# Softmax sums of 16 heads in one block, one reciprocal a batch, spread through DRAM; another opening order

## What is computed

```python
qp = q @ Wq.T
k, v = jnp.split(latent_kv @ Wkv_expand.T, 2, axis=-1)
scores = jnp.einsum('bhqd,bhkd->bhqk', qh, kh) * inv_sqrt_d
scores = jnp.where(causal, scores, jnp.finfo(scores.dtype).min)
attn = jax.nn.softmax(scores, axis=-1)
out = jnp.einsum('bhqk,bhkd->bhqd', attn, vh)          # heads concatenated after this
x = _layernorm(x + out @ Wout.T, axis=-1)
```

## Time and profile before

| | us |
|---|---|
| median of 3 runs (lowest to highest) | 1207.15 (1203.7 to 1211.64) |
| the profiled execution, device time | 1207.56 |
| its span, first to last instruction | 1205.9 |
| cross attention in it, about 288 to 626 | 338 |
| step 0, first `below_peak` to `attend(0)` (340.95 to 363.17) | 22.2 |
| step t = 1, start of `attend(0)` to `attend(1)` (363.17 to 399.30) | 36.1 |
| steps t = 2..5, from 399.30 to 548.29 | 149.0 |
| steps 6 and 7 | 31.3, 26.3 |

### The profile page before, as it was taken

How to read it: one execution, slowest core, us unless ns; L and a number is a source line. 1 busy time by engine, 2 the same in 40 slices (tenths; PEclk the granted TensorE clock), 3 DMA queues, 4 the chain that set the end, 5 groups by cost and what they waited for, 6 DMA issues and landing times. The chain is left out here.

```text
span 1205.9 us, 19206 instructions
## 1 busy us (share of the span) xinstructions
PE 1083.9 (90%) x6786; PEld 913.0 (76%) x6786; DVE 732.0 (61%) x1552; ACT 445.4 (37%) x795; POOL 286.2 (24%) x380
## 2 busy tenths in 40 slices
PE   5999999998498889887758969999999999899997
PEld 4788888886487677776636848999989999787785
DVE  3746374562676786677554746776767777434575
ACT  4614233242143333433325224555545555221210
POOL 4510101004222332223325211122111221223030
PEclk9999999999789999888888989999999999999998
DMA  4402020304878668564216137667766676432241
GB/s 148 167 1 105 0 104 0 104 0 153 247 219 229 180 179 215 159 168 132 72 58 213 31 118 251 220 226 244 241 241 214 230 236 214 139 106 94 80 140 70
DMA packets 88820, 179.33 MB, mean 149 GB/s; under 512 B 8032, under 2 KB 33632, under 8 KB 87104
## 3 DMA queue, kind: packets, MB, share of 16 engines
q1 hardware_dynamic: 82096, 155.06, 40.2%
q0 software_dynamic: 6672, 23.60, 5.8%
HBM read 136.95 MB, written 41.42 MB: 148 GB/s over the span
## 5 line engine op out<-in xcount | busy, mean ns | idle before, releaser
L45 PE MATMUL e_ps_h<-e_x_lo,e_gu_hi 128*128 128x256 f32 (+1 forms) x552 | 156.2, 283 | 5.0 <-DVE e_x_lo L1722 5.0
L46 PE MATMUL e_ps_h<-e_x_hi,e_gu_lo 128*128 128x256 f32 (+1 forms) x552 | 154.1, 279 | 0.0
L47 PE MATMUL e_ps_h<-e_x_hi,e_gu_hi 128*128 128x256 f32 (+1 forms) x552 | 154.0, 279 | 0.0
L45 PE MATMUL a_ps_proj<-a_x_lo,arena 128*128 128x512 f32 x256 | 102.8, 401 | 15.1 <-DVE a_x_lo L295 12.2
L740 DVE CUSTOM_DVE_ANT_0 b_dump<-b_ps_s,b_mask 128x128 f32<-128x128 f32 (+1 forms) x256 | 79.7, 352 | 55.7 <-PE b_ps_s L924 55.2
L45 PEld LDWEIGHTS e_ps_h<-e_x_lo,e_gu_hi 128*128 128x128 f32 (+1 forms) x552 | 99.6, 180 | 6.2 <-DVE e_gu_lo L1726 5.2
L309 DVE SCALAR_TENSOR_TENSOR a_xc<-a_ps_proj,a_taps,a_xc 128x510 f32<-128x510 f32 (+2 forms) x96 | 71.6, 746 | 53.4 <-ACT a_xc L268 51.1
L46 PE MATMUL a_ps_proj<-a_x_hi,arena 128*128 128x512 f32 x256 | 102.1, 399 | 0.0
L47 PE MATMUL a_ps_proj<-a_x_hi,arena 128*128 128x512 f32 x256 | 102.1, 399 | 0.0
L46 PEld LDWEIGHTS e_ps_h<-e_x_hi,e_gu_lo 128*128 128x128 f32 (+1 forms) x552 | 99.7, 181 | 1.0
L47 PEld LDWEIGHTS e_ps_h<-e_x_hi,e_gu_hi 128*128 128x128 f32 (+1 forms) x552 | 99.7, 181 | 0.0
(11 more groups left out here) (294 smaller groups left out, 2741.2 us busy)
## 6 DMA issues: line engine op xcount, KB each, us to landing
f_gate_up_raw<-we_gate_up SPq DMA_DIRECT2D x88, 352.0 KB, 4.8
qk_split<-arena SPq DMA_DIRECT2D x32, 512.0 KB, 4.8
b_sk<-qk_split SPq DMA_DIRECT2D x48, 256.0 KB, 4.1
b_sq<-qk_split SPq DMA_DIRECT2D x48, 256.0 KB, 5.5
f_down_raw<-we_down SPq DMA_DIRECT2D x23, 512.0 KB, 3.8
y_slots<-f_y_tile SPq DMA_DIRECT2D x23, 512.0 KB, 2.8
f_x_next<-x SPq DMA_DIRECT2D x6, 1024.0 KB, 6.4
f_down_raw<-we_down SPq DMA_DIRECT2D x23, 192.0 KB, 3.9
```

What stands on the lines that cost most here:

```text
L45: pe.matmul(out, a_hi, b_lo, start=first, stop=False)
L46: pe.matmul(out, a_lo, b_hi, start=False, stop=False)
L47: return pe.matmul(out, a_hi, b_hi, start=False, stop=last)
```

## The change

- `attend`: all row sums of a batch are computed first, 32 matmuls with weights `pick[:, c]`, whose ones stand in every fourth column from c on. Head h of chunk c adds its sums into partitions h*32 + c, h*32 + c + 4, ... of one 128x256 block in `ps_x`. Then 64 values x exp matmuls fill both blocks of `ps_o` with no wait on `normalize`.
- VectorE takes one reciprocal of 128x256 a batch (`invert`) instead of four. SP stores it to DRAM (`inverse`) and reads it back four times, each time 4 rows copied to 32 partitions, into `share` (128 x 4 x 256). This is `share_inverse(t-1)`, first in SP's step t.
- ScalarE copies the unnormalised output from PSUM to `a_raw` (`keep`); VectorE multiplies it by `share` in two halves of 128x512, in the next step at u = 0, i = 2 and 3. `a_hi` and `a_lo` follow in halves on ScalarE (i = 2, 3) and GpSimd (i = 4, 5). PE's `out` waits for them.
- `peaks(t, 1)` moves from i = 1 to i = 4 on PE and ScalarE, to i = 5 on VectorE. SP's place for its transfer stays.
- Opening: the statistics move behind `turned(1, 1)`; the four normalising instructions go to ScalarE at the end of step -1; batch 1's context is rounded a step earlier; GpSimd's memset of `sk` comes earlier.
- `split_stored` and `m_loaded` become single semaphores; `m_hi` and `m_lo` share a tile.

```diff
+            def share_inverse(b):
+                sp.wait_ge(rinv_done, b + 1)
+                sp.dma_start(inverse_dram, rinv[:]).then_inc(share_loaded, 16)
+                sp.wait_ge(share_loaded, 80 * b + 16)
+                if b:
+                    sp.wait_ge(a_raw_done, 2 * b)
+                for h in range(HC):
+                    rows = slice(h * HD, (h + 1) * HD)
+                    sp.dma_start(share[rows], inverse_dram[h * HD:h * HD + HC].rearrange("(o c) t -> o c t", o=1)
+                                 .broadcast_to([HD, HC, S])).then_inc(share_loaded, 16)
...
             for t in range(FIRST_T, END_T):
+                if 1 <= t <= B:
+                    share_inverse(t - 1)
                 if 0 <= t - 2 < NORMED:
...
                         cut(t, u, i)
+                        if t and u == 0 and i in (4, 5):
+                            rest(t - 1, i - 4)
...
+            def keep(b):
+                for u in range(2):
+                    act.wait_ge(sums_o_ready, o_count(b, u))
+                    if b:
+                        act.wait_ge(a_lo_done, 2 * (b - 1) + u + 1)
+                    act.activation(a_raw[:, UC * u:UC * u + UC].rearrange("p c t -> p (c t)"), ps_o[:, u], ACT.Copy)\
+                        .then_inc(o_kept, 1)
+
+            def attended(b, u):
+                act.wait_ge(a_raw_done, 2 * b + u + 1)
+                if b:
+                    act.wait_ge(out_ready, 2 * b)
+                cs = slice(UC * u, UC * u + UC)
+                act.activation(a_hi[:, cs], a_raw[:, cs], ACT.Copy).then_inc(a_hi_done, 1)
...
                     if t == -1:
+                        act.wait_ge(ln_step, TILES + 7)
+                        for k in range(TILES):
+                            act.activation(res[:, k], res[:, k], ACT.Identity, scale=left_ln.rstd[:, k:k + 1],
+                                           bias=left_bias[:, k:k + 1]).then_inc(normed_done, 1)
                         peaks(0, 0)
...
-                        if i == 1 and u == 0:
+                        if i == 4 and u == 0:
                             peaks(t, 1)
...
+                        if t and u == 0 and i in (2, 3):
+                            attended(t - 1, i - 2)
+                keep(t)
...
-            def normalize(b, c):
-                dve.wait_ge(o_ready, DC * b + c + 1)
-                if b:
-                    dve.wait_ge(a_lo_done, DC * (b - 1) + c + 1)
-                dve.reciprocal(rinv[:, c % 2], ps_o[:, c % 2, S:2 * S]).then_inc(rinv_done, 1)
-                dve.wait_ge(rinv_done, DC * b + c + 1)
-                dve.tensor_tensor(a_raw[:, c], ps_o[:, c % 2, 0:S], rinv[:, c % 2], ALU.mult).then_inc(a_raw_done, 1)
+            def invert(b):
+                dve.wait_ge(sums_o_ready, sums_count(b))
+                if b:
+                    dve.wait_ge(share_loaded, 80 * b)
+                dve.reciprocal(rinv[:], ps_x[:, 0, 0:S]).then_inc(rinv_done, 1)
+
+            def normalize(b, u):
+                dve.wait_ge(share_loaded, 80 * (b + 1))
+                dve.wait_ge(o_kept, 2 * b + u + 1)
+                a = a_raw[:, UC * u:UC * u + UC].rearrange("p c t -> p (c t)")
+                dve.tensor_tensor(a, share[:, UC * u:UC * u + UC].rearrange("p c t -> p (c t)"), a, ALU.mult).then_inc(a_raw_done, 1)
...
             def out(b, k, part):
                 t = b + 1
+                pe.wait_ge(a_lo_done, 2 * b + part + 1)
...
             def attend(b):
                 pe.wait_ge(cut_done, HEADS * (b + 1))
+                for c in range(DC):
+                    for r in range(BT):
+                        for h in range(HC):
+                            mm = pe.matmul(ps_x[h * HD:(h + 1) * HD, 0, r * P:S], pick[:, c],
+                                           pt[:, HC * c + h, 2 * r * P:(2 + r) * P],
+                                           start=c == 0 and r == 0, stop=c == DC - 1 and r == BT - 1)
+                mm.then_inc(sums_o_ready, 1)
                 pe.wait_ge(v_done, 2 * b + 2)
```

More of the change, by code:

```diff
@@ L410, in cross_attention @@
         mask = sb("mask", [P, 3 * P])
-        ones = sb("ones", [P, HD])
+        pick = sb("pick", [P, HC, HD])
+        share = sb("share", [P, DC, S])
         x_hi = sb("x_hi", [P, DC, S], F32R)
@@ L584, in cut, with rest @@
                                    pattern=[[0, 2], [1, P]], channel_multiplier=-1).then_inc(cut_done, 1)
-            def rest(b, c):
-                pool.wait_ge(a_hi_done, DC * b + c + 1)
-                pool.tensor_tensor(a_lo[:, c], a_raw[:, c], a_hi[:, c].bitcast(F32), ALU.subtract).then_inc(a_lo_done, 1)
+            def rest(b, u):
+                pool.wait_ge(a_hi_done, 2 * b + u + 1)
+                cs = slice(UC * u, UC * u + UC)
+                pool.tensor_tensor(a_lo[:, cs], a_raw[:, cs], a_hi[:, cs].bitcast(F32), ALU.subtract).then_inc(a_lo_done, 1)
             context(0)
@@ L598, in _ @@
                                    fill=MASKED, base=0, pattern=[[-1, P]], channel_multiplier=1).then_inc(consts, 1)
[L599 to L600 removed]
+            for c in range(HC):
+                pool.memset(pick[:, c, c:HD:HC], 1.0).then_inc(consts, 1)
+            pool.wait_ge(consts, 10)
             context(1)
@@ L613, in _ @@
                     pool.tensor_tensor(bln.rstd[:], bln.var[:], bln.power[:], ALU.pow).then_inc(rstd_done, 1)
-                for c in range(DC):
-                    rest(t, c)
+            for u in range(2):
+                rest(B - 1, u)
         @block.scalar
@@ L666, in fill @@
                         if i == 0:
-                            context(b)
+                            if b != 1:
+                                context(b)
                             turned(b, 0)
@@ L670, in fill @@
                             turned(b, 1)
+                            if b == 0:
+                                context(1)
                         if i == 2:
@@ L702, in _ @@
                             peaks(t + 1, 0)
-                for c in range(DC):
-                    act.wait_ge(a_raw_done, DC * t + c + 1)
-                    if t:
-                        act.wait_ge(out_ready, 2 * t)
-                    act.activation(a_hi[:, c], a_raw[:, c], ACT.Copy).then_inc(a_hi_done, 1)
+                        if t and u == 0 and i in (2, 3):
+                            attended(t - 1, i - 2)
+                keep(t)
+            for u in range(2):
+                attended(B - 1, u)
         @block.vector
@@ L797, in fill @@
                             norm_step(o, i - 3)
-            def left_sums():
-                moments(dve, res, left_ln, ln_step, 0, var_done)
-                dve.wait_ge(rstd_done, 1)
-                for k in range(TILES):
-                    dve.tensor_scalar(res[:, k], res[:, k], left_ln.mean[:, k:k + 1], left_ln.rstd[:, k:k + 1],
-                                      ALU.subtract, ALU.mult).then_inc(normed_done, 1)
             for u in range(2):
@@ L825, in _ @@
                         fill(t, u, i)
-                        if u == 0 and i == 1:
+                        if t and u == 0 and i in (2, 3):
+                            normalize(t - 1, i - 2)
+                        if u == 0 and i == 5:
                             peaks(t, 1)
@@ L829, in _ @@
                             peaks(t + 1, 0)
-                for c in range(DC):
-                    normalize(t, c)
+                invert(t)
+            for u in range(2):
+                normalize(B - 1, u)
             for k in range(BT):
@@ L955, in attend @@
                         pe.wait_ge(m_lo_done, 2 * b + 2)
[L956 removed]
+                    if c == UC and real(b + 1):
                         pe.wait_ge(m_lo_done, 2 * b + 3)
[L958 to L967 removed]
+                    if c % UC == 0 and b:
+                        pe.wait_ge(o_kept, 2 * (b - 1) + c // UC + 1)
+                    for r in range(BT):
+                        for h in range(HC):
+                            head = HC * c + h
+                            mm = pe.matmul(ps_o[h * HD:(h + 1) * HD, c // UC, c % UC * S + r * P:(c % UC + 1) * S],
+                                           v[:, b % 2, r, head * HD:(head + 1) * HD], pt[:, head, 2 * r * P:(2 + r) * P],
+                                           start=r == 0, stop=r == BT - 1)
+                    if c % UC == UC - 1:
+                        mm.then_inc(sums_o_ready, 1)
             def fill(t, u, i):
```

83 lines of the change are left out of this document (44 added, 39 removed).

## The result

| | before | after |
|---|---|---|
| median, us (lowest to highest) | 1205.68 (1203.70 to 1211.64) | 1252.76 (1248.02 to 1254.42) |
| the profiled execution, us | 1207.56 | 1248.02 |
| its span, us | 1205.9 | 1246.1 |
| last output projection begins, us | 617.41 | 657.38 |

The changed kernel is slower: ratio 1.0375, 95% interval 1.0327 to 1.0424. (The median of before is over four runs here; the table ahead of the prediction had three of them.) The profiled execution of after is the lowest of its four, so differences read from the two traces add up to 40.5 us where the medians stand 47.1 apart. All 40.0 us of the traces' difference are there when the last output projection begins, so the loss is inside cross attention.

What follows compares the result with a forecast made beforehand. PE, busy 90%, was taken to bound the kernel; the change adds a loop through SP of 11.6 + 11.8 + 14.2 + 5.2 = 42.8 us. Delays 38.9 + 3 + 2.6 = 44.5 on 1207.5 give 1252 us, range 1220 to 1268.

Steps and rivals of the forecast that it cites:

- term 1: SP's list, from the low part of peaks (t, 1) done to the first stack load: 11.6 us (10.7 to 12.4).
- term 2: SP's list, from the first to the second stack load of a step: 11.8 us, not getting shorter.
- term 3: From second stack load to `share` landed, the inverse store queued behind six stack pieces: 14.2 us (12.5 to 15.7).
- term 4: VectorE and ScalarE work from `share` landed to the low part of the next peaks: 5.2 us (4.7 to 6).
- tail: After `attend(7)` to the last projection: 14.1 us against 11.5 before, so +2.6 us.
- The loop through SP: Cross attention: peaks wait for `share`, `share` for SP behind stack loads, those for earlier peaks; 42.8 us for 36.5 us steps.
- Step 0: First cross-attention step, with two residuals queued: peaks to stack load 13.4 us, next peaks at 396.1.
- small transfers overtake: Rival: the round trip's small transfers pass the stack loads, each of six rounds 4.2 us shorter, 1227 us; chance 0.15.
- the round trip is hidden: Rival: `share` at most 8.6 us behind the stack load, so the kernel is faster, 1180 us; chance 0.11.
- The wait at the product: VectorE waiting on a DMA before its product with `share`: near 10 us in steps 1 to 6.
- The opening: Before step 0: PE's 13.44 us wait goes, but SP waits for `normed_done` before the stack load; gains about nothing.
- step 7: Cross-attention step with an empty queue: 16.2 us from `attend` to `out`, against 13, so +3 us.

## Why the prediction was right

The forecast was 1252 us in a range from 1220 to 1268, with 0.79 on slower by over 1%; the median is 1252.76. Its steps against the trace:

| | predicted | measured |
|---|---|---|
| term 1, peaks to first stack load | 11.6 | 10.6, 10.5 |
| term 2, first to second stack load | 11.8 | 12.1 |
| term 3, second stack load to `share` | 14.2 | 13.7 |
| term 4, `share` to the peaks | 5.2 | 5.2 |
| sum, steps 2 and 3 | 42.8 | 41.6, 42.0 |
| peaks (0, 1) issued | 351.5 | 353.77 |
| peaks (1, 1), (2, 1), (3, 1) | 396.1, 436.7, 479.5 | 397.83, 438.08, 479.72 |
| peaks (4, 1), (5, 1) | 522.3, 562.7 | 521.76, 561.78 |
| `out(5, 0, 0)` | 602.8 | 601.23 |
| tail, `attend(7)` to the last projection | 14.1 | 13.4 |

- **The loop through SP** is what the runs show. That the four terms add up to the step is no proof, since they are cut out of one round. What shows it is that in steps 1 to 6 of after SP never waits for the inverses, that nothing but the trip's place in SP's list changed where 46 us came back, and that SP then waits for the inverses in every step. Making the peaks early shortens the loop too, by 22 us in all.
- **Term 1** was 1 us too large, with 10.6 just under my lower bound of 10.7: the residual lands 6.4 us after its issue in this step, where it took 7.9 in the one stretch that I took the queue's pace from the earlier trace rows. With 0.5 us too much in term 3 it makes the steps 0.4 to 1.2 us shorter than forecast.
- **Step 0** was missed by 2.3 us: the late peaks (0, 1) go out at 353.77. They also make `attend(0)` start at 370.79, against 363.17 before and 361.94 with the peaks early. I had not priced this step. Its first term I put at 13.4, where the rows that I named add up to 13.9 (1.5 and 12.4); it measured 13.0. Behind it SP's loop takes over, and the five steps that were each a little shorter than forecast had used up the 2.3 us by the peaks (5, 1).
- **Term 3, the queue in order.** The store lands 5.8 us after its issue, behind the six pieces, as counted (9.7 less 3.9). Two small errors cancel in it: the row's 5.6 us is the median of two pieces, and the last one took 6.0 by itself (6.0 in after too), while the store follows it by 0.4 us and not by 0.8. The half microsecond too much is in the loads, which land 2.2 us behind their last issue (472.34 to 474.54), where I took 3.0. The rival "small transfers overtake" (1227) needed a landing within 3 us and is refuted; so is "the round trip is hidden" (1180), which needed `share` at most 8.6 us behind the stack load. The price of the Trainium skill's page "DMA: Bandwidth & Descriptors", section "Anatomy of one DMA", would have made term 3 9.5, as an estimate; the page gives it for transfers issued by GpSimd, and here SP issues. It is near what an empty queue shows: by it a store of 128 KB takes 2.3 us, and the last two stores of after land in 1.7 and 2.0; the whole trip would take 5.5, and took 5.8 with the trip first. The backlog has to be added.
- **The wait at the product** was foretold near 10 us in steps 1 to 6. It is 10.4 in the first and 5.5 to 7.3 in the other five: the place was right, the size was not.
- **The opening** gains nothing: measured by itself, ratio 0.9989. The reason that I gave (the stack load (1, 0) a little later) is in the trace, 330.14 against 328.36. The experiment with the store moved shows more: without SP's wait it would still not start before 326.4.
- **The clock.** I had the lower clock only at the upper end of the range. It fell, from 0.955 to 0.936 over the span. The trace cannot say what that cost.
- **The sum.** The traces stand 40.0 us apart at the last projection, the medians 47.1; my 44.5 lies between, so the agreement with the median to a microsecond is partly luck. Against the traces I was 4.5 too high: 1.6 at `out(5, 0, 0)` (+37.3 for +38.9), 2.3 behind it (up to `attend(7)` the loss grows by 0.7, to +38.0, where I had 3 for step 7), and 0.6 in the tail. Step 7 is the term of the sum that was mis-sized most: from `attend(6)` at 616.76 to its output projection at 631.48 are 14.7 us, not 16.2, and PE makes up most of the rest by `attend(7)`.

## What to carry to other kernels

Before adding a wait to an engine that issues transfers, write down everything that engine has to issue between this wait and the same wait of the next step, and follow it round through the engines that release it: where each idle stretch of the issuing engine is one of the loop's own waits, the sum of that loop, not the busy time, is the new step. A dependent round trip through memory belongs ahead of bulk transfers, in issue order and in time; here its place before or behind six loads of 256 KB was worth 46 us, or 30 with the peaks early. A second queue did not get round the backlog here, since its transfers meet the same transfer engines: 1242 us with it, 1207 with the trip first on the one queue.

## What was not expected of the hardware

- The backlog holds a small transfer up on another queue as well: a store of 128 KB landed in 5.2 us on ScalarE's own queue, with the stack pieces of SP's queue in flight, against 5.8 on SP's queue and 1.7 to 2.2 with two pieces or nothing in flight.
- Two pieces of 256 KB put ahead of four loads of 128 KB, with four behind, made the time from the store's issue to the product 2.8 us longer. I had expected 1 to 2.
- Four such loads took ScalarE 2.79 us to issue while the engines were full (1.73 on SP, and 1.8 on ScalarE in the step where its first load went out at 498.85), and its next exponential started 5.18 us after its idle time began, 2.3 of them before the first issue.
- Not settled: in which order the transfer engines serve the two queues. The store at 455.42 landed in the order of issue across both; the one at 496.64 passed a piece issued 1.3 us before it. The loads issued on ScalarE's queue from 498.85 on, beside the stack pieces of SP's, needed 8.9 us to `share`. What makes the difference the traces do not show.
